# Negated-maximum products in 32-row tiles, issued beside the low and the high maximum product

## What is computed

```
xn = _layernorm(x, axis=-1)
...
scores = jnp.einsum('bhqd,bhkd->bhqk', Qr, Kr) / HEAD_DIM ** 0.5
weights = jax.nn.softmax(scores, axis=-1)
out = jnp.einsum('bhqk,bhkd->bhqd', weights, V_rep)
...
x = x + _L0_attn_ref(xn, ...) + _L0_ffn_ref(xn, ...)
```

## Time and profile before

| | us |
|---|---|
| median of 3 runs | 615.31 |
| profiled execution | 615.39 |
| its span | 613.5 |
| TensorE busy | 548.0 (89%) |
| VectorE busy | 398.9 (65%) |
| ScalarE busy | 380.9 (62%) |

### The profile page before, as it was taken

One profiled execution on the slowest core, in us unless ns is written; L12 is line 12 of the kernel. 1 busy time (PEld: TensorE's weight loads), 2 busy tenths in 40 slices (PEclk: granted clock), 3 DMA queues, 4 the chain that ended last, 5 costly groups with the idle time before them and its releaser, 6 DMA issues.

```text
span 613.5 us, 10690 instructions
## 1 busy us (share of the span) xinstructions
PE 548.0 (89%) x3288; PEld 272.0 (44%) x3289; DVE 398.9 (65%) x904; ACT 380.9 (62%) x548; POOL 172.7 (28%) x208
## 2 busy tenths in 40 slices
PE   2996757997499899999999999999999999999997
PEld 1932333454255444444444444444444444444443
DVE  4378754942146666777778787788787788874113
ACT  3421412332033333799889888989988988886572
POOL 3014844532022110003415421641354232500000
PEclk9997976999699999999999999999999999999999
DMA  9930235558521211310411321312115103000101
GB/s 297 378 122 0 81 140 160 168 192 203 146 86 53 66 38 36 96 35 19 123 43 47 102 52 55 83 52 77 44 53 131 40 20 87 18 2 20 43 26 52
DMA packets 38272, 53.52 MB, mean 87 GB/s; under 512 B 6144, under 2 KB 24448, under 8 KB 38240
## 3 DMA queue, kind: packets, MB, share of 16 engines
q1 hardware_dynamic: 31344, 40.26, 22.6%
q0 software_dynamic: 3408, 9.31, 5.5%
q10 hardware_dynamic: 3488, 3.55, 1.7%
HBM read 36.18 MB, written 16.65 MB: 86 GB/s over the span
## 4 chain that ended last, share of the span: by engine, by line
PE 69%; DVE 14%; DMA 6%; issue 5%; SPq 3%; POOL 2%; ACT 1%; DVEq 0%; ACTq 0%; POOLq 0%
PE bank L1258 16%; PE bank L1248 10%; PE bank L1250 10%; PE bank L1116 9%; PE bank L1180 6%; DMA k_st<-rope_low 4%; PE bank L1130 4%; PE bank L1197 4%; DVE xn_t L919 3%; PE bank L1282 3%; PE bank L1128 2%; PE bank L1076 2%; DMA rows_out<-xn 1%; DVE xn L842 1%; SPq L403 1%
## 5 line engine op out<-in xcount | busy, mean ns | idle before, releaser
L712 ACT ACTIVATE big<-bank 128x1024 f32<-128x1024 f32 x256 | 247.9, 1025 | 17.6 <-PE bank L1250 17.6
L1258 PE MATMUL bank<-big,v_st 128*32 128x512 f32 x1024 | 136.4, 605 | 0.0
L916 DVE TENSOR_REDUCE mx<-bank 128x1 f32<-128x512 f32 x128 | 88.3, 689 | 56.4 <-PE bank L1130 45.7
L1248 PE MATMUL bank<-ms,ones_r 64*128 64x512 f32 x512 | 103.4, 399 | 0.4 <-ACT big L712 0.4
L911 DVE TENSOR_REDUCE mx<-bank 128x1 f32<-128x512 f32 x128 | 88.5, 691 | 22.8 <-PE bank L1118 17.8
L1250 PE MATMUL bank<-qs,kb 64*128 64x512 f32 x512 | 101.4, 391 | 0.0
L664 ACT ACTIVATE xn_t<-bank 128x512 f32<-128x512 f32 x128 | 76.6, 598 | 38.4 <-PE bank L1118 34.3
L1180 PE MATMUL bank<-big,xn 128*128 x156 | 80.8, 643 | 16.3 <-ACT xn L678 15.8
L919 DVE CUSTOM_DVE_ANT_0 xn_t<-bank,xn_t 128x512 f32<-128x512 f32 x128 | 87.1, 681 | 0.0
L1116 PEld LDWEIGHTS bank<-ka,qs 64*128 64x128 f32 x128 | 23.4, 183 | 114.9 <-DVE mx L916 77.8
L1116 PE MATMUL bank<-ka,qs 64*128 64x512 f32 x128 | 63.3, 494 | 11.6 <-DVE mx L919 10.0
(11 more groups left out here) (142 smaller groups left out, 607.9 us busy)
## 6 DMA issues: line engine op xcount, KB each, us to landing
qs<-q_hl SPq DMA_DIRECT2D x64, 128.0 KB, 2.7
rows_out<-xn SPq DMA_DIRECT2D x39, 128.0 KB, 1.9
ka<-k_st SPq DMA_DIRECT2D x16, 256.0 KB, 4.3
kb<-k_st SPq DMA_DIRECT2D x16, 256.0 KB, 4.1
xs<-in_L_attn_x SPq DMA_DIRECT2D x4, 512.0 KB, 6.4
big<-in_L_ffn_Wg SPq DMA_DIRECT2D x16, 128.0 KB, 6.0
big<-in_L_ffn_Wu SPq DMA_DIRECT2D x16, 128.0 KB, 6.0
big<-in_L_ffn_Wd SPq DMA_DIRECT2D x16, 128.0 KB, 5.8
```

The source lines that it names most:

```text
L712: act.activation(probs[kt % 2][:, 2 * j:2 * j + 2, :].rearrange("p r q -> p (r q)"), st_ps[j][:, :], ACT.Exp, scale=1.0 / math.sqrt(HD)).t ...
L916: nc.vector.reduce_max(mx[h][:, STEPS + k, 1:2], mx_ps[i % 3], axis=X_AXIS).then_inc(mx_taken, 1)
L1248: mm(out[i], ones_r[half[i], :], ms[v][half[i], j, :], start=True, stop=False)
L1258: last = mm(o_ps[32 * r:32 * (r + 1), :], v_st[p][:, kt, :], probs[kt % 2][:, r, :], start=(kt == 0), stop=(kt == KT - 1))
```

## The change

`ms` loses its dimension for the half j: its 512 columns now hold one half of the queries, and the two halves stand in different rows, half 0 in rows 64 to 127 and half 1 in rows 0 to 63; within these, the two query pairs s are 32 rows apart (`shift_row`). So a shift product has a contraction of 32 rows and is a tile of 32 by 128, and the two of one half take the 64 rows that one maximum product leaves free. `score_first` is cut in two: `score_low` stands ahead of the shifts of half 0, `score_high` ahead of those of half 1. SyncE sends 8 transfers of half the size per round. The diff, cut to its core:

```diff
-        ms = [sb(f"ms{p}", [P, 2, HALF], F32R) for p in range(2)]
+        ms = [sb(f"ms{p}", [P, HALF], F32R) for p in range(2)]
...
+        def shift_row(j, s):
+
+            return STACK * (1 - j) + STACK // 2 * s
...
-                for s in range(2):
-                    for row, part in ((STACK * s, m_hi), (STACK * s + 1, m_lo)):
-                        sp.dma_start(ms[i][row:row + 1, :, :].rearrange("o j (t c) -> o (j t) c", c=P).bitcast(F32),
-                                     part[i][STEPS * s:STEPS * (s + 1), :].bitcast(F32)).then_inc(m_loaded[i], 16)
+                for j in range(2):
+                    for s in range(2):
+                        for row, part in ((shift_row(j, s), m_hi), (shift_row(j, s) + 1, m_lo)):
+                            sp.dma_start(ms[i][row:row + 1, :].rearrange("o (t c) -> o t c", c=P).bitcast(F32),
+                                         part[i][STEPS * s + QT * j:STEPS * s + QT * (j + 1), :].bitcast(F32)).then_inc(m_loaded[i], 16)
...
-            def score_first(v, q, p, k, ready=None):
+            def score_low(v, q, p, k, ready=None):
...
+            def score_high(v, q, p, k):
...
-            def scores(q, v, p, kt, s, j):
+            def shifts(v, s, j):
+
                 if s is not None:
                     pe.wait_ge(exp_done, 2 * (s - 1) + j + 1)
...
                 for i in range(2):
-                    mm(out[i], ones_r[half[i], :], ms[v][half[i], j, :], start=True, stop=False)
+                    row = shift_row(j, i)
+                    mm(st_ps[j][:, i * HALF:(i + 1) * HALF], ones_r[row:row + STACK // 2, :], ms[v][row:row + STACK // 2, :],
+                       start=True, stop=False)
...
-                            score_first(u + 2, ahead, 1 - p, kt, before_first(u + 2, kt))
...
                         for j in range(2):
+                            if not last:
+                                if j == 0:
+                                    score_low(u + 2, ahead, 1 - p, kt, before_first(u + 2, kt))
+                                else:
+                                    score_high(u + 2, ahead, 1 - p, kt)
                             if kt < KT - 1:
-                                scores(2 * p + h, h, p, kt + 1, s + 1, j)
+                                shifts(h, s + 1, j)
+                                scores(2 * p + h, p, kt + 1, j)
...
```

More of the change, by code:

```diff
@@ L506, in _ @@
             for m in ms:
-                pool.memset(m[:, :, :].bitcast(F32), 0.0).then_inc(stacks_padded, 1)
+                pool.memset(m[:, :].bitcast(F32), 0.0).then_inc(stacks_padded, 1)
             pool.memset(ones_r[:, :].bitcast(F32), 1.0).then_inc(stacks_padded, 1)
@@ L1014, in group @@
                         if k == 0:
-                            split_maxima(u + 1, 1 - h, scored(u + 2, TURN), None if begun else 64 * (g + h))
+                            split_maxima(u + 1, 1 - h, scored(u + 2, TURN), None if begun else 128 * (g + h))
                     turn_output(u, first and h == 0)
@@ L1023, in _ @@
             invert_sums(u - 1)
-            split_maxima(u + 1, 1, NI * (u + 2), 64 * (G - 1))
+            split_maxima(u + 1, 1, NI * (u + 2), 128 * (G - 1))
             def finish(n):
@@ L1114, in score_first @@
                     pe.wait_ge(mx_taken, ready)
-                low, high = mx_ps[i % 3], mx_ps[(i + 1) % 3]
-                mm(low.rearrange("p (c n) -> p c n", c=2), qs[q][0:STACK, j, rows], ka[p][0:STACK, :, QUART:HALF],
+                mm(mx_ps[i % 3].rearrange("p (c n) -> p c n", c=2), qs[q][0:STACK, j, rows], ka[p][0:STACK, :, QUART:HALF],
                    start=True, stop=True).then_inc(mx_scored, 1)
-                mm(high.rearrange("p (c n) -> p c n", c=2), qs[q][STACK:P, j, rows], ka[p][STACK:P, :, 0:QUART],
+            def score_high(v, q, p, k):
+                i, j, rows = first_use(k) + 1, k // QT, slice(k % QT * P, (k % QT + 1) * P)
+                mm(mx_ps[i % 3].rearrange("p (c n) -> p c n", c=2), qs[q][STACK:P, j, rows], ka[p][STACK:P, :, 0:QUART],
                    start=True, stop=True).then_inc(mx_scored, 1)
@@ L1155, in first_max @@
                 if n % 2 == 0:
-                    score_first(v, v, 0, k, before_first(v, k) if v or k else None)
+                    score_low(v, v, 0, k, before_first(v, k) if v or k else None)
+                    score_high(v, v, 0, k)
                 else:
@@ L1238, in _, with scores @@
             down(SLOTS - 1, (SLOTS - 1) % 4, False, last_y_ps)
-            def scores(q, v, p, kt, s, j):
+            def shifts(v, s, j):
                 if s is not None:
                     pe.wait_ge(exp_done, 2 * (s - 1) + j + 1)
-                out = [st_ps[j][:, i * HALF:(i + 1) * HALF] for i in range(2)]
-                half = [slice(STACK * i, STACK * (i + 1)) for i in range(2)]
-                keys = slice(kt % QT * P, (kt % QT + 1) * P)
                 for i in range(2):
-                    mm(out[i], ones_r[half[i], :], ms[v][half[i], j, :], start=True, stop=False)
+                    row = shift_row(j, i)
+                    mm(st_ps[j][:, i * HALF:(i + 1) * HALF], ones_r[row:row + STACK // 2, :], ms[v][row:row + STACK // 2, :],
+                       start=True, stop=False)
+            def scores(q, p, kt, j):
                 for i in range(2):
-                    last = mm(out[i], kb[p][half[i], kt // QT, keys], qs[q][half[i], j, :], start=False, stop=True)
+                    half, keys = slice(STACK * i, STACK * (i + 1)), slice(kt % QT * P, (kt % QT + 1) * P)
+                    last = mm(st_ps[j][:, i * HALF:(i + 1) * HALF], kb[p][half, kt // QT, keys], qs[q][half, j, :],
+                              start=False, stop=True)
                 last.then_inc(st_ready, 1)
@@ L1262, in _ @@
             pe.wait_ge(kb_loaded[0], 32)
-            pe.wait_ge(m_loaded[0], 64)
-            scores(0, 0, 0, 0, None, 0)
+            pe.wait_ge(m_loaded[0], 128)
+            shifts(0, None, 0)
+            scores(0, 0, 0, 0)
             pe.wait_ge(y_copied, SLOTS)
-            scores(0, 0, 0, 0, None, 1)
+            shifts(0, None, 1)
+            scores(0, 0, 0, 1)
             def project_tile(t, chunks):
@@ L1307, in group @@
                         if kt == KT - 1 and h == 0:
-                            pe.wait_ge(m_loaded[1], 64 * (g + 1))
+                            pe.wait_ge(m_loaded[1], 128 * (g + 1))
                         if kt == KT - 1 and h == 1 and not last:
                             pe.wait_ge(kb_loaded[1 - p], 32 * ((g - p) // 2 + p) + 32)
-                            pe.wait_ge(m_loaded[0], 64 * (g + 2))
+                            pe.wait_ge(m_loaded[0], 128 * (g + 2))
                         for j in range(2):
+                            if not last:
[3 more added lines that the diff above has]
+                                    score_high(u + 2, ahead, 1 - p, kt)
                             if kt < KT - 1:
-                                scores(2 * p + h, h, p, kt + 1, s + 1, j)
+                                shifts(h, s + 1, j)
+                                scores(2 * p + h, p, kt + 1, j)
                             elif h == 0:
-                                scores(2 * p + 1, 1, p, 0, s + 1, j)
+                                shifts(1, s + 1, j)
+                                scores(2 * p + 1, p, 0, j)
                             elif not last:
-                                scores(2 * (1 - p), 0, 1 - p, 0, s + 1, j)
+                                shifts(0, s + 1, j)
+                                scores(2 * (1 - p), 1 - p, 0, j)
                         if not last:
```

## The result

The changed kernel takes 734.04 us (median of 5 runs, 731.91 to 770.89) against 613.09 of the kernel before (median of 5, 610.85 to 617.3). The ratio is 1.1931, with a 95% interval of 1.1878 to 1.1985: 19% slower, some 121 us. The forecast was 739. Two of the five runs (770.89 and 750.0) had a lower mean granted clock, 0.918 and 0.950 against 0.972 to 0.977, and are left out of the ratio.

The account below looks back on a forecast made before the run. TensorE's stream and a ring through ScalarE's gain were both taken to bind at 2.61 us per step. Adding 114.2 (steps), 8.7 (last two rounds) and 0.6 (half steps) to 615.4 gave 739 us; range 613 to 760.

Parts of the forecast that it names:

- TensorE's stream: Groups of products TensorE runs per attention step; said to reach the second maximum pair at 1.26 of a 2.61 us step.
- the ring through the gain: Per step, low maximum product, ScalarE's gain, second maximum pair, values, next low product: a chain of waits of 2.61 us.
- The price of a change: On TensorE, each tile-size change costs 0.10 us leaving, 0.11 entering; assumed also for 64 to 32 rows; chance 0.54.
- An ordinary step: Attention step with maximum products: low to values 2.63 us in place of 1.61, +1.02, over 112 steps 114.2 us.
- The long steps: Steps around a round's start, 3.07 us, waiting for VectorE's last reduction; to grow by the same amount as others.
- the last two rounds: 15 steps with shifts but no maximum products: 1.14 us to become 1.72, +0.58 each, 8.7 us.
- ahead of the rounds: Two half steps ahead of the loop, claimed to add 2 x 0.3 = 0.6 us.
- SyncE's transfers: 8 transfers for 4 per round, +2.5 us on SyncE's queue; cost 0, at most 40 us if the cover were gone.
- Overlapping rows alone: Rival: low and high run beside shifts, size changes in the same rows still cost; +0.38 per step, 667 us; chance 0.15.
- No price: Rival: 64-to-32-row changes cost nothing, but the ring keeps ordinary steps from gaining; 620 us; chance 0.25.
- the 4.5 us for the late high product: Within the no-price rival: high issued 0.57 later delays VectorE's reductions in some steps, 2.3 + 2.2 = 4.5 us.
- Faster: Rival: no price and the gain not the holder, so steps fall from 2.61 to 2.43; 595 us; chance 0.06.

Follow-up runs that it names:

- f_gain: The kernel before with ScalarE's gain taken of 128 of its 512 columns, all six groups kept: 607.81 us, ratio 0.9927.
- d_five: The kernel before with the second shift pair left out, so five groups of 64-row tiles per step: 608.18 us, ratio 0.9942.
- e_five_gain: The kernel before without the second shift pair and with the gain taken of 128 of its 512 columns: 580.94 us, ratio 0.9459.
- a_height: The changed kernel with low and high side by side again ahead of the first shifts, shifts still 32 rows: 707.67 us, ratio 1.1537.
- g_twice: The changed kernel with each pair of shift products issued twice in a row into its bank: 820.39 us, one run, mean clock 0.937.
- c_four: As a_height, but all four 32-row shifts of a step together, behind the first pair and ahead of both score pairs: 650.64 us, ratio 1.0576.
- b_order: The kernel before with the changed kernel's order (low and high apart) but its own 64-row shifts: 618.19 us, ratio 1.0079.
- h_bank: The kernel before, a round's first maximum pair waiting for one reduction less of the round before: 607.04 us, ratio 0.9882.

## Why the prediction was right

*The bound.* TensorE's stream and the ring through the gain both end at 2.61 us in a step. f_gain, d_five and e_five_gain show the two separately: with the ring shortened the stream gives 2.59, with the stream shortened the ring gives 2.61, with both shortened the step is 2.36.

*The price of a change.* This was the open point: no row showed 64 against 32 rows, and I took the price of the other changes, 0.10 for leaving and 0.11 for entering. The rows after show it on four changes per step, as low and the shifts stand one behind the other in different rows (0.43). a_height shows it without the new order, g_twice that it belongs to the change and not to the tile, c_four that it is paid once for four tiles. The forecast took the full price over from changes with a 128-row tile and gave it 0.54; that it holds here is measured, why the array does not run the two heights side by side is not. That the full price, including 0.10 and the load that is not ahead, appears at a pure change of rows among fp32r products also rules out that the type had been paid for in the earlier trace rows.

*The sum.* An ordinary step was to grow by 1.02; it grew by 1.00 (3.61 for 2.61; the scores with what follows took 0.66 instead of 0.67, twice). The long steps, forecast to grow alike, did: 462.04 to 466.11, 4.07 for 3.07. Not every step grew by as much: the first of the rounds took 3.90 already before and takes 4.06, and the 12 ordinary steps that took 2.70 before grew by 0.91. From the first low product of the rounds to the last, the 111 steps take 412.7 us (253.71 to 666.45) where they took 304.2 (251.26 to 555.46): 108.5 more, where 111 x 1.02 is 113.2. From there to the end it is 9.7 more: one step, and 8.7 for the last two rounds, which went from 1.14 to 1.72, exactly the +0.58 forecast, 15 times. The last 2.5 of the 120.7 by which the spans differ (734.2 and 613.5) lie ahead of the rounds, where 0.6 was forecast; in the traces of these kernels the first low product of the rounds starts anywhere from 246.8 to 253.7, so that much tells nothing. SyncE's transfers were given nothing, and no shift product of the trace is listed as waiting for a transfer.

*The rivals.* Overlapping rows alone (667): falsified by low and the shifts, whose rows do not overlap and which did not run together. No price (620): falsified, but both of its mechanisms were seen apart, the ring that gives nothing back in d_five and the 4.5 us for the late high product in b_order (5). Faster (595): it needed low to be done earlier or the gain not to be asked for; e_five_gain, with the gain shortened, comes nearest to that case and is faster by 5%. The range, 613 to 760, reached down to the kernel before, so that the measured time lies in it says little; the 0.43 from low to the shifts and the 1.72 in the last two rounds are what bears the forecast out.

*What was off.* The forecast is 5 us over the measured median: the sum was 2.8 too high (123.5 for 120.7): 4.7 too high for the 111 steps, of which 0.02 in each comes of the stretches between changes and the rest of the steps that took more than 2.61 or 3.07 before; and 1.9 too low ahead of the rounds, which is scatter as far as is known. The other 2.3 are that the profiled execution it starts from (615.4) lies above the median of the five runs of before (613.09). The expectations of b_order (an idle group that did not appear) and of c_four (a ring through ScalarE that I had not seen) missed, each for a reason of its own, not of the theory's price. That of h_bank had the size but not the way.

## What to carry to other kernels

Count the changes of tile size in TensorE's program, not only the groups: each cost 0.20 us here, nearly the 0.23 of a whole group of 512 columns, and small tiles of another height do not fill the rows that a larger one leaves free. Gather tiles of one height, as four 32-row tiles cost as much as two where nothing waited for a bank. Before removing work from a stream that looks full, follow the chain of waits round one step and add it up; if it comes to the same period, both have to be shortened, and c_four shows that a reordering can build a new ring.

## What the runs showed of the hardware that was not expected

The clock. The kernel before did not leave the full level in the attention of its trace. The changed kernel did, in the run of 770.89 us, though TensorE was busy for 9.61 us of the 10 ahead of the fall, no less than elsewhere. Windows of 10 us (busy us of each engine and count, granted clock, DMA share, GB/s):

```profile
330.00:340.00 10.00, 9.61 (x56) 3.38 (x48) 5.79 (x13) 6.73 (x9) 0.00 (x0) 1.00 0.17 52
...
350.00:360.00 10.00, 10.00 (x32) 3.62 (x31) 2.68 (x5) 4.39 (x6) 4.89 (x6) 0.50 0.09 26
...
370.00:380.00 10.00, 9.61 (x56) 3.40 (x55) 6.79 (x14) 7.18 (x8) 0.61 (x1) 1.00 0.29 79
```

At 0.50 (1.2 GHz) a group between two changes took 0.73 rather than 0.43 (355.72 low, 356.44 shifts, 357.17 scores). What the engine did before the fall is the same sequence of steps as elsewhere, with six changes of size in each. g_twice, with as many, fell too (0.937 over its one run). But a_height also has six in a step and held 0.973 to 0.978 in its four runs, and f_gain, with the two of the kernel before, had one run of twelve with a mean of 0.933, of which no trace tells where it fell. Whether the changes of size have a part in it stays open; it was not tested.

Also new to me: two halves of the array can run skewed by a group against each other, at 2.61 us per step, with tiles of one height (b_order).
